# Adding the second expert's result during the load: a DMA with addition in place of a VectorE addition

## The reference

```
x = x + deltanet(layernorm(x))          # a gated delta rule over chunks of 64 tokens, 4 heads
x = x + experts(layernorm(x))           # 8 experts 128 -> 512 -> 128, each token goes to its best 2
x = x + recurrence(layernorm(x))        # exp/sigmoid gates, a linear scan over the tokens, a division
x = x + experts(layernorm(x))
```

```
topk_probs, topk_idx = top_k(softmax(xf @ router_w.T), 2)
out = gelu(xf @ w_fc[e] + b_fc[e]) @ w_proj[e] + b_proj[e]      # for every expert e
y   = out[first choice] * weight + out[second choice] * weight
```

## Time and profile before

| | |
|---|---|
| median of three runs | 1839.96 us (1839.38 to 1845.61) |
| the profiled execution | 1818.88 us |
| its span, first to last instruction | 1817.1 us |
| busy: TensorE | 64% |
| busy: VectorE | 65% |
| busy: ScalarE | 38% |
| busy: GpSimd | 45% |
| additions of results on VectorE | 32, of 1.20 to 1.23 us |
| loads of results | 32, of 512 KB |

### The profile page before, as it was taken

The page is one execution under the profiler, slowest core; times in us unless marked ns, Lnnn a source line. Parts: engine busy times, 40 slices in busy tenths (PEclk is TensorE's granted clock), DMA queues, the critical chain, the costliest instruction groups (busy, mean ns, idle before and its releaser), DMA issues.

```text
span 1817.1 us, 33396 instructions
## 1 busy us (share of the span) xinstructions
PE 1163.0 (64%) x12131; PEld 841.3 (46%) x12131; DVE 1174.8 (65%) x3241; ACT 698.5 (38%) x1478; POOL 812.5 (45%) x695
## 2 busy tenths in 40 slices
PE   4556575756574545259999935655665439999930
PEld 1234443434343434148888713443443328888720
DVE  1489857675767743348888727777775448888642
ACT  3333423323231211147777623322322027777620
POOL 3223434343535143336666621455555335666550
PEclk9777675858575555579999965555555559999975
DMA  3111011110101000267767411111000066777636
GB/s 97 44 36 38 27 37 32 33 32 33 33 31 40 27 28 18 62 226 249 250 242 252 165 69 47 38 51 50 28 27 32 26 206 240 250 248 247 230 102 186
DMA packets 83797, 186.69 MB, mean 103 GB/s; under 512 B 18288, under 2 KB 48178, under 8 KB 73650
## 3 DMA queue, kind: packets, MB, share of 16 engines
q1 hardware_dynamic: 64400, 148.55, 24.4%
q0 software_dynamic: 18176, 35.72, 5.7%
q10 hardware_dynamic: 1058, 0.29, 0.1%
HBM read 131.15 MB, written 56.98 MB: 104 GB/s over the span
## 4 chain that ended last, share of the span: by engine, by line
PE 46%; DVE 23%; issue 12%; POOL 7%; ACT 5%; DMA 3%; another core or an unknown queue 2%; SPq 1%; POOLq 0%; ACTq 0%; DVEq 0%
PE ps L1360 5%; PE ps L1568 4%; PE ps L1570 4%; PE ps L1569 4%; PE ps L1582 4%; PE ps L1580 3%; PE ps L1581 3%; DVE seq L1024 3%; PE ps L1463 3%; PE ps L1636 3%; PE ps L1637 2%; PE ps L1501 2%; POOL xs L561 2%; ACT ysc L1079 2%
## 5 line engine op out<-in xcount | busy, mean ns | idle before, releaser
L599 POOL DMA_INDIRECT res<-orow,idt x312 | 328.5, 1053 | 226.2 <-issue 113.6
L561 POOL DMA_INDIRECT xs<-ysc,slot_u x256 | 267.5, 1045 | 264.7 <-DVE slot_u L843 193.5
L948 DVE TENSOR_TENSOR hidl<-hidf,hidh 128x512 fp32r<-128x512 f32 x312 | 215.2, 693 | 65.8 <-ACT hidh L1257 58.0
L1255 ACT ACTIVATE hidf<-ps,wb 128x512 f32<-128x512 f32 x312 | 209.4, 704 | 8.6 <-remote 4.3
L1568 PE MATMUL ps<-yTh,wb 128*128 128x512 f32 x312 | 130.9, 419 | 0.5 <-ACT hidh L1257 0.4
L1580 PE MATMUL ps<-hidh,wb 128*128 128x512 f32 x312 | 130.3, 417 | 0.0
L1079 ACT ACTIVATE ysc<-x,r_shift,r_rstd 128x128 f32<-128x128 f32 x128 | 51.0, 480 | 195.4 <-POOL r_shift L534 195.4
L1570 PE MATMUL ps<-yTh,wb 128*128 128x512 f32 x312 | 123.8, 397 | 0.0
L1569 PE MATMUL ps<-yTl,wb 128*128 128x512 f32 x312 | 123.8, 397 | 0.0
L1582 PE MATMUL ps<-hidh,wb 128*128 128x512 f32 x312 | 123.6, 396 | 0.0
L1581 PE MATMUL ps<-hidl,wb 128*128 128x512 f32 x312 | 123.1, 394 | 0.0
(11 more groups left out here) (231 smaller groups left out, 2785.1 us busy)
## 6 DMA issues: line engine op xcount, KB each, us to landing
wb<-wblob SPq DMA_DIRECT2D x78, 1032.0 KB
xt<-xs SPq DMA_DIRECT2D x78, 288.0 KB
wblob<-hl SPq DMA_DIRECT2D x16, 512.0 KB, 3.0
hidf<-res SPq DMA_DIRECT2D x16, 512.0 KB
rs<-res SPq DMA_DIRECT2D x16, 512.0 KB
res<-orow,idt POOLq DMA_INDIRECT x312
xs<-filler SPq DMA_DIRECT2D x17, 288.0 KB, 5.1
x<-in_hidden SPq DMA_DIRECT2D x64, 64.0 KB, 1.9
```

Of the source, the lines that this page charges most:

```text
L561: pool.indirect_dma_start(xs[:, :], bass.IndirectOffsetOnAxis(slot_u[:, g % 2, k, n:n + 1], 0), ysc[:, g % 2, n, :], None).then_inc(s(f"mo ...
L599: pool.indirect_dma_start(res[m][:, :], bass.IndirectOffsetOnAxis(idt[:, t % IR, j:j + 1], 0), orow[:, t % 2, j, :], None, bounds_check=2 ...
L948: ve.tensor_tensor(hidl[:, t % 2, c, :], hidf[:, c, :], hidh[:, t % 2, c, :].bitcast(F32), ALU.subtract)\
L1255: ins = act.activation(hidf[:, c, :], ps[:, c, :], ACT.Gelu_apprx_tanh, bias=b_col)
```

## The change

SP loads only the first result into `rs[b % 2][:, 0]`. GpSimd waits for that load and then issues a DMA of the second result from DRAM onto the same place, with addition. VectorE waits for that DMA and adds only once, into x. For batches 0 and 1 GpSimd's new issues stand before the first power of the third layer, for batches 2 to 7 in the turn two batches earlier, after the sends of block 5, and for batches 8 to 15 after the last put of the second expert layer.

```diff
@@ results_sync (SP)
-                    for k in range(2):
-                        by_row = res[m][k * B * L:(k + 1) * B * L, :].rearrange("(p n) c -> p n c", p=P)
-                        sp.dma_start(rs[b % 2][:, k], by_row[:, b % B * BPB:(b % B + 1) * BPB, :])\
-                            .then_inc(s(f"r_in{b % 2}"), 16)
+                    by_row = res[m][0:B * L, :].rearrange("(p n) c -> p n c", p=P)
+                    sp.dma_start(rs[b % 2][:, 0], by_row[:, b % B * BPB:(b % B + 1) * BPB, :])\
+                        .then_inc(s(f"r_in{b % 2}"), 16)
@@ GpSimd, third layer
+            def second_choice(b):
+                by_row = res[b // B][B * L:2 * B * L, :].rearrange("(p n) c -> p n c", p=P)
+                pool.wait_ge(s(f"r_in{b % 2}"), 16 * (b // 2 + 1))
+                pool.dma_start(rs[b % 2][:, 0], by_row[:, b % B * BPB:(b % B + 1) * BPB, :], accum_op=ALU.add)\
+                    .then_inc(s(f"r_both{b % 2}"), 16)
+
             def linrec_power(b):
...
+            second_choice(0)
+            second_choice(1)
             linrec_power(0)
             for b in range(B + 1):
                 for n in range(BPB):
...
                     if n == 2 and b + 1 < B:
                         linrec_power(b + 1)
+                    if n == 5 and b + 2 < B:
+                        second_choice(b + 2)
             for n in range(BPB):
                 send(2 * B - 1, n)
             moe_pool(1)
+            for b in range(B, 2 * B):
+                second_choice(b)
@@ add_results (VectorE)
-                ve.wait_ge(s(f"r_in{b % 2}"), 16 * 2 * (b // 2 + 1))
+                ve.wait_ge(s(f"r_both{b % 2}"), 16 * (b // 2 + 1))
                 xb = x[:, b % B * BPB:(b % B + 1) * BPB, :]
-                ch.link(ve.tensor_tensor(rs[b % 2][:, 0], rs[b % 2][:, 0], rs[b % 2][:, 1], ALU.add))
                 ins = ve.tensor_tensor(xb, xb, rs[b % 2][:, 0], ALU.add)
```

## The result

The changed kernel takes 1851.71 us (median of 10 runs, 1848.1 to 1858.67), the kernel before on the same chip 1837.48 (10 runs, 1825.09 to 1851.97): a ratio of 1.0095, 95% interval 1.0068 to 1.0121, so slower by about 17 us (12 to 22). The forecast was 1848.1, a range of 1841 to 1865, and chances of 0.47 for no change and 0.51 for slower. The single time came out 4 us from the forecast, but the change itself did not: +8.1 was forecast and about +17 measured.

The account below looks back on a forecast made before the run. No engine was full; the chain of loads and additions, then 64 stores, set the end. Terms +6.8 + 2.6 - 1.25 = +8.1 us gave 1827.0 from the profiled 1818.88, or 1848.1 from the 1839.96 median; range 1841 to 1865.

Parts of the forecast that it names:

- the end: Adding the second expert layer's results, batches 8 to 15, then the output stores: forecast +6.8 us.
- rival B: At the end, the engines' adding is its own bound, a quarter of the copy's rate: +21.8, 1862 us; chance 0.30.
- What bounds the end: Batches 8 to 15: the moment batch 13 is added sets the end, as 64 stores follow the last load; +7.2.
- Load and issue: In one buffer's turn at the end: 3.6 us for the 512 KB load, 0.98 for GpSimd's issue.
- Data of an accumulation, twice the copy's: Within the landing: the accumulation also reads its destination, so 512 KB takes 2.6 us where a copy takes 1.3.
- rival C: An accumulation is as fast as a copy, with a put's fixed part, 2.3 us to landing: 1840 us; chance 0.15.
- Fixed part: From the end of GpSimd's issue to landing, the time outside the data: taken as 1.5 us.
- Sharing: In the end turns: the engines' share of a pair of batches, 7.8 us, still fits in the 10.1 us cycle.
- Stores: After the last load at the end: 64 stores issued in 31.49 us before; one SP issue fewer ahead, -0.4.
- Head: Start of the third layer, batch 0: load, GpSimd's issue, landing and one addition in series, +2.6 us.
- Batch 1's addition: Third layer, inside the first batch's work on the chain: one VectorE addition removed counts in full, -1.25 us.
- Steady turns: Third layer, batches 2 to 7: the copy of the logits waits anyway, so removing additions gains and costs 0.

Follow-up runs that it names:

- the copy in series: The changed kernel with GpSimd's transfer as a plain copy, still after the load, the results' addition left out: 1841.73 us, ratio 1.0018 to the kernel before.

## Why the prediction was right or wrong

The direction, the place and the range were right; the sum was +8.1, and what the stages show is +18.7: the end +16.0, the head +3.2, batch 1 -0.5. That the single time still came within 4 us is in part luck: the forecast was added to a median of three runs, 1839.96, and ten runs of the same kernel gave 1837.48. The stages' sum lies nearer to rival B's +21.8 than to the forecast's +8.1, but B's cause, a quarter of the rate, is not what the traces show (below). The chance of slower was barely above that of no change, and the measured change is clear of the 9.2 us that I took as the bound.

- **What bounds the end:** right. The moment when batch 13 is added and the 64 stores behind it set the end. Batch 15's addition, over at 1824, still had room before its stores.
- **Load and issue:** forecast 3.6 and 0.98; measured 3.9 to 4.0 from SP's issue to GpSimd's, where 3.7 was forecast with the wake-up, and 0.84 to 0.86 in the turns (up to 1.00 elsewhere). Right to 0.3.
- **Data of an accumulation, twice the copy's:** right, and now shown: 3.3 against 1.65 us of all engines, and a landing of 4.4 against 3.4 when only the addition is taken out. The Trainium skill's rule in "Collectives: The Full Stack" (Part 3, why ReduceScatter is half of AllGather) gives this factor; the traces here agree, with 3.3 / 1.65 = 2.0 and, when the engines are full, 388 / 181 = 2.1. Rival B's 6.7 and rival C's 2.3 to landing are both excluded by 4.4 to 4.7 for an accumulation alone.
- **Fixed part:** 1.5 forecast. A copy alone lands in 3.3 to 3.4, which with the forecast's 1.3 of data leaves 2.0 to 2.1, and with the 1.65 of the windows 1.7. By this estimate the term was 0.2 to 0.6 short. The estimate of 3.2 from the Trainium skill's "DMA: Bandwidth & Descriptors" (Anatomy of one DMA) fits the copy's 3.3 from the end of GpSimd's issue (from its start it is 3.9 to 4.0); for the accumulation, for which I had weighed it, it is 1.2 to 1.5 too low.
- **Sharing, the step that failed:** I wrote that the engines' share of a pair, 7.8, still fits in a turn, and took from this that it costs nothing. The share was too low to begin with: it measures 9.9, nearly all of the 10.1 that I gave a turn. And a transfer can fit on the average and still stand behind another one; I had counted that for batch 9 in the first turn (5.6 to landing, 6.0 measured), but not in the turns after it. Landing is 4.65 alone and 6.2 to 6.8 in the turns. Two turns measured 24.9 instead of 20.2, +4.7. The addition of batch 13 came 12.5 us later after the first load than before, instead of 7.2; the remaining 0.6 lies in the first turn.
- **Stores:** not foreseen. I subtracted 0.4 for the missing load issue and left the 64 stores at 31.5. They took 35.5 beside two accumulations, 32.3 beside two copies of the same size, 33.0 beside one accumulation. That is +4.0.
- **Head:** +2.6 forecast, +3.2 measured; landing 4.42 against 4.1, and the load 0.3 slower.
- **Batch 1's addition:** -1.25 forecast. From the end of batch 0's addition to that of batch 1's it is 24.3 to 25.6 in five kernels with two additions and 23.0 to 24.5 in eight with one; the means differ by 1.1. In the profiled pair only 0.5 of it shows.
- **Steady turns, nothing:** right. The copy of the logits waits 1.3 longer, and comes at the same 14.70. The six turns take 44.8 on average before and 45.2 after; over all kernels it is 44.1 to 45.4 with the old form and 43.5 to 45.4 with the new one.

So the term that was mis-sized is the landing in the turns (6.5, not 4.1) and a term for the stores was missing; the chain of load, issue, accumulation and addition, and the twofold reading, were those of the forecast. How much of the 6.5 comes from the other buffer's load and how much from its accumulation stays open.

## What to carry to other kernels

A DMA that adds moves the work of a short VectorE instruction (1.22 us here) into a transfer that needs twice the engines' time and must wait for the first load, so I would expect it to pay only where VectorE bounds and the landing is hidden (batch 1's 1.1 us is the one gain seen here), and it is dear in a chain of load, add, load. When two buffers alternate, a landing time measured alone is too low for the turns: add what the other buffer's transfers need from the same engines, with their engine time taken from a trace, and do not count on a sum of shares that just fits. And look behind the last load: 64 stores that only waited for SP's turn were worth 18 us of the end (60.1 to 41.8), more than the change cost there (16.0).

## What was not expected of the hardware

- Beside accumulations SP's issue of plain stores slowed down: six issues in 6.82 us, where 0.49 each is the mean in the kernel before. Beside plain copies of the same size by GpSimd it was 32.3 for all 64, against 35.5. It is not the accumulations alone: with stores between plain loads, and no accumulation, one issue took 1.35. Why the issue and not only the landing is slower stays open.
- GpSimd needs 0.84 to 1.00 us to issue a direct accumulation of 128 rows of 4 KB and 0.53 to 0.60 for the copy in series.
- In one turn an accumulation's last bytes seem to straggle. Windows of half a microsecond around the end of batch 11's accumulation in the changed kernel, columns as above:

```profile
1794.50:1795.00 0.50, 0.00 (x0) 0.00 (x0) 0.22 (x1) 0.00 (x0) 0.00 (x0) 0.50 0.88 172
1795.00:1795.50 0.50, 0.00 (x0) 0.00 (x0) 0.50 (x1) 0.00 (x0) 0.00 (x0) 0.50 0.19 33
1796.00:1796.50 0.50, 0.00 (x0) 0.00 (x0) 0.01 (x1) 0.00 (x0) 0.00 (x0) 0.50 0.13 25
```

The bulk is over at 1795.0, a share of 0.13, two engines' worth, goes on to 1796.5, and VectorE starts at 1797.25. That these bytes are the accumulation's is inferred: the next load was issued only at 1796.03. A plain load was seen by VectorE about 1 us after its bytes had stopped. Which engines are late, and why, was not examined, nor whether other turns show it.
